# Involution block on one core: the convolution in eight parts of two channel groups by four images, in place of four parts of one group by eight images

## The chip, the cores and the metric

The kernel runs on one core of a Trainium2 chip. The metric is device time in microseconds (us). Engines in the text: PE (matmuls), PEld (its weight loads), DVE (vector), ACT (scalar), POOL (GpSimd), SP (here it only issues DMAs). A core has 16 DMA engines that move what all queues ask for.

## The reference

The input x has 16 images of 64 channels, 56 x 56 pixels. The block adds an involution (a 7 x 7 convolution whose weights are made per pixel from the normalised input) and then a mixture of experts, two of eight per token.

```
r   = relu(batchnorm(conv1x1(ln_c(x), w1) + b1))          # 16 channels
ker = conv1x1(r, w2) + b2                                 # 16 groups x 49 taps per pixel
for i in range(7):
    for j in range(7):                                    # 4 channels of a group share a tap
        out += shifted(ln_c(x), i, j) * ker[:, :, i*7 + j]
x = x + out
t = tokens(x)                                             # 50176 tokens of 64
top_w, top_i = top_k(ln_t(t) @ Wg + bg, 2)                # 8 experts
t = t + sum over the two of w * (gelu(ln_t(t) @ W1[e] + b1[e]) @ W2[e] + b2[e])
```

All arithmetic is float32.

## The kernel before

Four stages follow one another: normalisation (it writes the normalised maps to a DRAM tensor `xs`, the reduced channels to `rs`, and the tap weights to `vf`), the convolution with the gate, the experts, and a merge. The change is in the first two.

**Convolution.** `STEPS` = 64 steps, t = 0 to 63. A step takes one of the four quarters (`QUARTERS`: upper or lower half of the rows, even or odd images; 16 steps each) and one channel group g = t % 16 (4 channels) of the quarter's 8 images. SP loads per step one `band` tile (`load_band`, L846: 119 partitions of 238 floats, the group's taps from `vf`; the source is written as 17 rows by 7 columns of 952 bytes) and three strips of the maps (`load_maps`, L856: 112 partitions of 8192 bytes each at L867, and a seventeenth row of 7 partitions at L870 for the first strip). There are 3 band buffers (`BR`) and 8 strip buffers (`XR`); a load waits until PE has read the buffer's last content. Strips and band of the first kind are split into two float32r parts: the high parts on ACT (L965 band, L972 maps), the low parts on DVE (L1144, L1147, in `low_parts` after the fourth unit of the step before). PE's `filters` then makes 8 units of matmuls (L1069 to L1075), DVE's `weigh` multiplies each unit with `r_all` (L1158), PE's `sums` adds them up (L1088), ACT evacuates (`evacuate`, L984) and stores to `co` (L990, one DMA of 128 partitions).

**Gate.** `CHUNKS` = 56 chunks of 896 tokens, 14 per quarter. `step_of(n)` puts chunk n at step 16 * (n // 14 + 1) + 2 + n % 14: a quarter's chunks are gated while the next quarter is convolved, and those of the last quarter in steps 66 to 79, after the convolution. A chunk is loaded by SP (`load_chunk`, from x and `co`; the first of a quarter waits until all stores of that quarter have landed), multiplied on PE (`unit`, L1103, in the step after the second unit, so PE waits there for the load), read out by ACT and ranked on DVE. Two chunks make a batch (28 in all), ranked one step after its second chunk and placed another step later; then POOL writes the batch's rows to `token_rows` with 14 indirect DMAs (L951). POOL does nothing else there, but for 28 earlier DMAs that fill `packs`.

Every queue works in order of the program: what stands behind a waiting instruction waits too. SP's order per step t is band and strips of step t + 1, then the chunk of step t.

The first stage stores the normalised maps with `xs_map` (L265, L316) inside a hardware loop (`rounds`, L320) on SP.

Of the kernel before, what the change touches and what calls it, by code (L numbers as in the profile page):

```python
# [79 lines left out]
QUARTERS = ((0, 0), (0, 1), (1, 0), (1, 1))  # L80
HALF = HALF_ROWS * W
QUARTER_CHUNKS = CHUNKS // len(QUARTERS)
BAND_LEAST = [min(IN0[r] - MROWS * m for r in strips for m in STRIP_BLOCKS[r]) for strips in STRIP_SETS]
BN = MF + MROWS * F

# [95 lines left out]
def norm_stage(nc, x, conv_w1, conv_b1, gamma, beta, conv_w2, conv_b2, xs, rs, ones_rows, vf,  # L181
# [11 lines left out]
    with ExitStack() as ctx:  # L193
# [68 lines left out]
        counted = sem("counted")  # L262
        packed = sem("packed")

        xs_map = xs[0:XS_SIZE].rearrange("(i h c x) -> i c h x", i=PARITY, h=H, c=C)  # L265
        vf_map = vf[:].rearrange("(g j t f) -> g j t f", g=G, j=K, t=TL)
        w2_map = conv_w2.rearrange("(i j g) c -> i g j c", i=K, j=K)
        b2_map = conv_b2.rearrange("(i j g u) -> i g j u", i=K, j=K, u=1)
# [7 lines left out]
        @block.sync  # L276
        def _(sp):
            x_pairs = x.rearrange("(p i) c h w -> p (i c) (h w)", i=PARITY)
            def load(pair):

                if pair >= 2:
                    sp.wait_ge(x_in[pair % 2], pair // 2 * 16)
                sp.dma_start(xin[:, pair, :], x_pairs[pair]).then_inc(x_in[pair % 2], 16)

            load(0)
            load(1)


            sp.wait_ge(cleared, 3)
            sp.dma_start(vf[:].rearrange("(p x) -> p x", p=P), zeros[:, :]).then_inc(blanks_done, 16)  # L290
            sp.dma_start(xs[XS_SIZE:XS_SIZE + WP].rearrange("(a x) -> a x", a=1),
                         zeros[0:1, 0:WP]).then_inc(blanks_done, 16)
            sp.dma_start(ones_rows.rearrange("j (x w) -> (j x) w", w=P8 * W),
                         ones[:, :]).then_inc(blanks_done, 16)
            load(2)
            load(3)

            def step(it, k):
                if isinstance(it, int) and it == 0 and k % 2 == 0:
# [14 lines left out]

                for i in range(PARITY):
                    sp.dma_start(xs_map[i][:, PAIR_ROWS * u:PAIR_ROWS * (u + 1), bass.ds(j * 2 * WP, 2 * WP)],  # L316
                                 xpad[u][C * i:C * (i + 1), :, :, :].rearrange("c h p w -> c h (p w)")
                                 ).then_inc(xs_out[u], 16)

            rounds(sp, STEPS, PER, 3, step)  # L320

            sp.wait_ge(blanks_done, 3 * 16)
            sp.wait_ge(filters_out, 2 * K * 16)
            for i in range(2):
                sp.wait_ge(rs_out[i], STEPS // 4 * 4 * 16)
            for u in range(UNITS):
                sp.wait_ge(xs_out[u], P8 // 2 * PARITY * 16)
# [366 lines left out]
def conv_gate_stage(nc, x, xs, rs, ones_rows, vf, co, affine, pick, tables, token_rows, tile_table,  # L694
# [8 lines left out]
    with ExitStack() as ctx:  # L703
# [7 lines left out]
        xq = [sb(f"xq{i}", [KP, XN]) for i in range(XR)]  # L711
        xq_hi = [sb(f"xq_hi{i}", [KP, XN], F32R) for i in range(2)]
        xq_lo = [sb(f"xq_lo{i}", [KP, XN], F32R) for i in range(2)]
        band = [sb(f"band{i}", [KP, BN]) for i in range(BR)]
        band_hi = [sb(f"band_hi{i}", [KP, BN], F32R) for i in range(2)]
        band_lo = [sb(f"band_lo{i}", [KP, BN], F32R) for i in range(2)]
# [99 lines left out]
        def quarter_of(t):  # L816
            return QUARTERS[t // G]

        def strip_of(t, i):
            return STRIP_SETS[quarter_of(t)[0]][i]  # L820

# [8 lines left out]
        R_STEPS = (0, 0, 4, 9, 25)  # L830
        R_NEED = (0, 0, G, 2 * G, 3 * G)
        def step_of(n):
            return G * (n // QUARTER_CHUNKS + 1) + 2 + n % QUARTER_CHUNKS

        def placing_step(b):
            return step_of(BATCH * b + BATCH - 1) + 2
# [8 lines left out]
        @block.sync  # L845
        def _(sp):  # L846
            def load_band(t):
                s, g = quarter_of(t)[0], t % G
                if t >= BR:
                    sp.wait_ge(b_lo, t - BR + 1)  # L850
                    sp.wait_ge(z_done, NU * (t - BR) + NU)
                src = bass.AP(vf, g * V_G + (TAP0 + PAD - (MROWS - 1) + BAND_LEAST[s]) * F,
                              [[F, max(KR)], [V_J, K], [1, BN]])
                sp.dma_start(band[t % BR][:, :], src).then_inc(band_in[t % BR], 16)

            def load_maps(t, i):  # L856
                n = GS * t + i
                slot, r = n % XR, strip_of(t, i)
                if n >= XR:
# [5 lines left out]
                par, g, top = quarter_of(t)[1], t % G, IN0[r]  # L865
                base = (par * H + top) * XS_H + g * XN
                sp.dma_start(xq[slot][0:16 * K, :],  # L867
                             bass.AP(xs, base, [[XS_H, 16], [1, K], [1, XN]])).then_inc(x_in[slot], 16)
                if i == 0:
# [12 lines left out]
                             ).then_inc(r_in[part], 16)  # L882

            def load_chunk(n):
                if n % QUARTER_CHUNKS == 0:
                    for i in range(2):
                        sp.wait_ge(ob_out[i], (n // QUARTER_CHUNKS + 1) * G // 2 * 16)
                if n >= XC:
                    sp.wait_ge(unit_done, n - XC + 1)
                for img, at, to, size in pieces(n):  # L890
                    sp.dma_start(xc[n % XC][0:C, to:to + size],
                                 x[img].rearrange("c h w -> c (h w)")[:, at:at + size]).then_inc(xc_in[n % XC], 16)
                    sp.dma_start(xc[n % XC][C:2 * C, to:to + size],
                                 conv_run(co, img, at, size)).then_inc(xc_in[n % XC], 16)
# [64 lines left out]
        @block.scalar  # L959
        def _(act):  # L960
            def split_band(t):
                act.wait_ge(band_in[t % BR], (t // BR + 1) * 16)
                if t >= 2:
                    act.wait_ge(z_done, NU * (t - 2) + LAST_UNIT[0] + 1)
                nc.scalar.activation(band_hi[t % 2][:, :], band[t % BR][:, :], ACT.Copy).then_inc(b_hi, 1)  # L965

            def split_maps(t):
                slot = GS * t % XR
# [11 lines left out]

            def evacuate(t):
                act.wait_ge(summed, t + 1)
                act.wait_ge(ob_out[t % 2], t // 2 * 16)
# [4 lines left out]
                dst = co[s, par, t % G].rearrange("i d q (h w) -> (q h) (i d) w", w=W)  # L988
                act.wait_ge(ob_done, t + 1)
                act.dma_start(dst, ob[t % 2][:, :].rearrange("p (e w) -> p e w", w=W)).then_inc(ob_out[t % 2], 16)  # L990

            def take_unit(n):
                b, k = divmod(n, BATCH)
# [56 lines left out]
        def _(pe):  # L1050
            def filters(t, u):
# [10 lines left out]
                for lot, (m, q) in enumerate(parts):  # L1062
                    zt = z_ps[(NU * t + u) % 3][0:MF, lot, 0:CN]
                    at = window(t, m, r)
                    if i == 0:
                        maps = [part[t % 2][rows_in, :].rearrange("p (d i w) -> p d i w", d=D, i=P8)[
                            :, :, 2 * q:2 * q + 2, 0:W] for part in (xq_hi, xq_lo)]
                        hi, lo = (part[t % 2][rows_in, at:at + MF] for part in (band_hi, band_lo))
# [69 lines left out]
        def _(dve):  # L1138
            def low_parts(t):
                slot = GS * t % XR  # L1140
                dve.wait_ge(b_hi, t + 1)
                if t >= 2:
                    dve.wait_ge(z_done, NU * (t - 2) + LAST_UNIT[0] + 1)
                nc.vector.tensor_tensor(band_lo[t % 2][:, :], band[t % BR][:, :],  # L1144
                                        band_hi[t % 2][:, :].bitcast(F32), ALU.subtract).then_inc(b_lo, 1)
                dve.wait_ge(x_hi, t + 1)
                nc.vector.tensor_tensor(xq_lo[t % 2][:, :], xq[slot][:, :],  # L1147
                                        xq_hi[t % 2][:, :].bitcast(F32), ALU.subtract).then_inc(x_lo, 1)
# [1 line left out]
            def weigh(t, u):  # L1150
                i, ((m, q), (m1, _)) = UNITS_OF[quarter_of(t)[0]][u]
                par = quarter_of(t)[1]
                dve.wait_ge(z_done, NU * t + u + 1)
                if m1 != m:
                    by = r_all[:, m:m + 2, par, 2 * q * W:2 * (q + 1) * W]
                else:
                    by = r_all[:, m, par, 2 * q * W:2 * (q + 2) * W].rearrange("p (m x) -> p m x", m=2)
# [554 lines left out]
```

## Time and profile before

| | us |
|---|---|
| median of 3 runs | 2265.68 |
| lowest and highest | 2265.55, 2266.97 |
| profiled execution | 2268.61 |
| its span, first to last instruction | 2266.7 |
| busy PE, DVE, ACT, POOL in the span | 1932.9, 1516.8, 785.9, 970.3 |
| mean granted clock of PE | 0.914 |

The profiled execution is 2.9 us above the median; 1.9 us of it lie outside its span. In a row of the profile an engine's idle time before an instruction stands in brackets with the instruction or DMA that ended it. SP rows are DMA issues: their duration is the time that the issue itself took on the queue. DMA share is the mean busy share of the 16 DMA engines, so a single busy engine shows as 0.06. Granted clock 1.00 is 2.4 GHz, 0.50 is 1.2 GHz.

### The profile page before, as it was taken

Reading aid. Unit: us, or ns where it says so; the run is one execution under the profiler, and the core shown is the slowest. Engines: PE = TensorE matmul, PEld = TensorE weight load, DVE = VectorE, ACT = ScalarE, POOL = GpSimd, SP = SyncE. Lnnn points to the kernel's source line nnn. Section 1 sums busy time; section 2 is a strip of 40 time slices with the busy share of each in tenths; the row PEclk is TensorE's granted clock in tenths of the full one; section 3 lists DMA queues with packets and bytes.
Section 4 is the critical chain, followed back from the end, with each engine's and each line's share of the span. In section 5 each row is a group of like instructions: output and inputs, shape, how many; then the busy total and the mean of one; then the engine's idle time right before and its main releaser. Section 6 shows DMA issues by size and latency. Waiting matters only on the chain. (4 is left out here: it accounts for less than half of the span.)

```text
span 2266.7 us, 32062 instructions
## 1 busy us (share of the span) xinstructions
PE 1932.9 (85%) x10208; PEld 1045.7 (46%) x10208; DVE 1516.8 (67%) x2682; ACT 785.9 (35%) x1382; POOL 970.3 (43%) x1038
## 2 busy tenths in 40 slices
PE   8975898887999999999999995307999999999945
PEld 5753444344555545555555554303444444444424
DVE  4444566565888877989878897634666666666634
ACT  4431111111223222232223323214666666666620
POOL 8001000100225350443505346773777777777740
PEclk9987999898999999999999995557999999999977
DMA  9767888887888777888778853234666566666439
GB/s 301 163 131 191 201 203 205 205 200 196 211 214 212 208 204 207 226 222 211 203 195 230 215 134 105 72 93 124 176 168 169 166 167 170 166 166 174 117 120 349
DMA packets 265820, 418.92 MB, mean 185 GB/s; under 512 B 116224, under 2 KB 188452, under 8 KB 242685
## 3 DMA queue, kind: packets, MB, share of 16 engines
q1 hardware_dynamic: 160701, 348.14, 57.8%
q0 software_dynamic: 32352, 39.58, 6.5%
q10 hardware_dynamic: 72608, 29.25, 5.5%
q8 instruction: 79, 1.29, 0.2%
q14 instruction: 80, 0.66, 0.1%
HBM read 337.34 MB, written 89.60 MB: 188 GB/s over the span
## 5 line engine op out<-in xcount | busy, mean ns | idle before, releaser
L951 POOL DMA_INDIRECT token_rows<-gate_rows,gate_index x392 | 414.9, 1059 | 663.4 <-DVE gate_index L1280 549.7
L1158 DVE TENSOR_TENSOR prod<-z_ps,r_all 119x896 f32<-119x896 f32 x512 | 543.5, 1083 | 130.8 <-PE z_ps L1071 100.8
L1474 POOL DMA_INDIRECT mixed<-exp_mix,exp_xt x474 | 478.0, 1008 | 175.3 <-issue 132.1
L1075 PE MATMUL z_ps<-xq,band 112*119 112x448 f32 x1024 | 442.4, 568 | 68.8 <-DVE prod L1158 68.7
L1492 ACT ACTIVATE exp_hid<-exp_h_ps,exp_pack 128x384 f32<-128x384 f32 x632 | 329.6, 574 | 242.2 <-PE exp_h_ps L1528 242.2
L1075 PEld LDWEIGHTS z_ps<-xq,band 112*119 112x119 f32 x1024 | 183.7, 189 | 277.3 <-issue 178.6
L1528 PE MATMUL exp_h_ps<-exp_tok,exp_pack 64*128 64x384 f32 x1264 | 248.9, 512 | 10.7 <-issue 10.4
L984 ACT ACTIVATE ob<-o_ps 128x448 f32<-128x448 f32 x64 | 34.8, 544 | 609.6 <-PE o_ps L1088 609.6
L1088 PE MATMUL o_ps<-prod,pick 119*32 119x448 f32 x2048 | 240.1, 562 | 1.2 <-DVE prod L1158 0.3
L1536 PE MATMUL exp_y_ps<-exp_hid,exp_pack 128*64 128x384 f32 x1264 | 238.8, 499 | 0.0
L1069 PE MATMUL z_ps<-xq_hi,band_hi 119*119 119x448 f32 x512 | 207.5, 405 | 23.7 <-DVE xq_lo L1147 20.7
L1570 DVE COPY exp_tok<-exp_x_ps 64x384 f32<-64x384 f32 x158 | 86.8, 550 | 166.8 <-PE exp_x_ps L1516 164.1
L1070 PE MATMUL z_ps<-xq_lo,band_hi 119*119 119x448 f32 x512 | 190.1, 371 | 0.0
L1071 PE MATMUL z_ps<-xq_hi,band_lo 119*119 119x448 f32 x512 | 189.2, 370 | 0.0
L1147 DVE TENSOR_TENSOR xq_lo<-xq,xq_hi 119x2048 fp32r<-119x2048 f32 x64 | 146.3, 2285 | 56.6 <-ACT xq_hi L972 56.6
L1103 PE MATMUL u_ps<-moe_gate_rhs,gate_xc 128*128 128x72 f32 x784 | 120.3, 317 | 74.0 <-issue 46.1
L1069 PEld LDWEIGHTS z_ps<-xq_hi,band_hi 119*119 119x119 f32 x512 | 94.4, 184 | 133.4 <-issue 115.9
L1103 PEld LDWEIGHTS u_ps<-moe_gate_rhs,gate_xc 128*128 128x128 f32 x784 | 116.7, 231 | 82.2 <-issue 52.0
L1528 PEld LDWEIGHTS exp_h_ps<-exp_tok,exp_pack 64*128 64x128 f32 x1264 | 111.2, 187 | 79.1 <-issue 39.3
L1576 DVE TENSOR_SCALAR exp_ysb<-exp_y_ps,exp_pack 64x384 f32<-64x384 f32 x158 | 98.6, 624 | 69.0 <-PE exp_y_ps L1536 68.1
L972 ACT ACTIVATE xq_hi<-xq 119x2048 fp32r<-119x2048 f32 x64 | 121.6, 1900 | 54.5 <-DMA xq<-xs 54.4
L1516 PE MATMUL exp_x_ps<-ident,exp_xt 128*64 128x128 f32 x474 | 82.8, 284 | 51.6 <-DMA exp_xt<-token_rows 51.6
(196 smaller groups left out, 2019.1 us busy)
## 6 DMA issues: line engine op xcount, KB each, us to landing
xq<-xs SPq DMA_DIRECT2D x192, 896.0 KB
exp_pack<-packs SPq DMA_DIRECT2D x158, 258.5 KB
exp_xt<-token_rows SPq DMA_DIRECT2D x158, 120.0 KB
xs<-xpad SPq DMA_DIRECT2D x32, 448.0 KB, 5.9
co<-ob ACTq DMA_DIRECT2D x64, 224.0 KB, 16.7
xin<-in_x_dram SPq DMA_DIRECT2D x8, 1568.0 KB, 11.2
merge_yt<-mixed ACTq DMA_DIRECT2D x28, 448.0 KB, 6.0
mixed<-exp_mix,exp_xt POOLq DMA_INDIRECT x474
```

The costliest lines, as they stand in the source:

```text
L951: pool.indirect_dma_start(out=token_rows[:, :], out_offset=bass.IndirectOffsetOnAxis(ap=index[b % RR][:, j:j + 1], axis=0), in_=rows[b % R ...
L1069: nc.tensor.matmul(zt, hi, maps[0], start=True, stop=False)
L1070: nc.tensor.matmul(zt, hi, maps[1], start=False, stop=False)
L1071: mm = nc.tensor.matmul(zt, lo, maps[0], start=False, stop=True)
L1075: mm = nc.tensor.matmul(zt, band[t % BR][rows_in, at:at + MF], maps, start=True, stop=True)
L1088: mm = nc.tensor.matmul(o_ps[32 * q:32 * (q + 1), 0:CN], pick[:, cols], prod[(NU * t + u) % PR][:, lot, :], start=i == 0 and lot == 0, sto ...
L1103: mm = nc.tensor.matmul(u_ps[:, GATE_COLS * j:GATE_COLS * (j + 1)], xc[n % XC][:, P * j:P * (j + 1)], tab.gate_rhs[:, :], start=True, stop ...
L1158: nc.vector.tensor_tensor(prod[(NU * t + u) % PR][:, :, :].rearrange("p m (d x) -> p m d x", d=D), z_ps[(NU * t + u) % 3][0:MF, :, 0:CN].r ...
L1474: pool.indirect_dma_start(out=mixed[:, :], out_offset=bass.IndirectOffsetOnAxis(ap=xt[t % XT][:, j, ROW_ID:ROW_ID + 1].bitcast(U32), axis= ...
L1492: nc.scalar.activation(hid[n % 8][:, :], h_ps[n % HT][:, 0:N], ACT.Gelu, bias=pack[t % WT][:, at:at + 1]).then_inc(gelu_done, 1)
L1528: nc.tensor.matmul(h_ps[n % HT][:, 0:N], pack[t % WT][half, P * blk:P * (blk + 1)], tok[t % 3][half, :], start=True, stop=True).then_inc(h ...
L1536: mm = nc.tensor.matmul(y_ps[t % 2][C * e:C * (e + 1), 0:N], pack[t % WT][:, at:at + C], hid[(t * 4 + 2 * blk + e) % 8][:, :], start=blk = ...
```

## The change

A quarter is halved into two sides of four images, so there are eight parts of 8 steps and 7 chunks each. A step takes two channel groups (twins) of four images; it has as many output values as before. `xs` is laid out so that a strip's 8192 bytes hold 8 channels of 4 images. A step now needs the bands of two groups: two band DMAs of the old size into a tile twice as wide, and the high and low split of 476 columns in place of 238. Chunk n is gated at step 8 * (n // 7 + 1) + 2 + n % 7: the first chunk moves from step 18 to step 10, the last from step 79 to step 72. The store to `co` becomes two DMAs of 64 partitions. Waits on all stores of a part come eight times in place of four. The loop of SP in the first stage is written out.

```diff
+SIDES = 2
+SIDE_CHUNKS = QUARTER_CHUNKS // SIDES
+TWINS = G // 2
+SIDE_X = P8 // SIDES * WP
...
-        xs_map = xs[0:XS_SIZE].rearrange("(i h c x) -> i c h x", i=PARITY, h=H, c=C)
+        xs_map = xs[0:XS_SIZE].rearrange("(i h a c x) -> i a c h x", i=PARITY, h=H, a=SIDES, c=C)
...
-                    sp.dma_start(xs_map[i][:, PAIR_ROWS * u:PAIR_ROWS * (u + 1), bass.ds(j * 2 * WP, 2 * WP)],
+                    at = j % (P8 // SIDES // 2) * 2 * WP
+                    sp.dma_start(xs_map[i, j // (P8 // SIDES // 2)][:, PAIR_ROWS * u:PAIR_ROWS * (u + 1), at:at + 2 * WP],
...
-            rounds(sp, STEPS, PER, 3, step)
+            for n in range(STEPS + 3):
+                step(*divmod(n, PER))
...
-        band = [sb(f"band{i}", [KP, BN]) for i in range(BR)]
+        band = [sb(f"band{i}", [KP, 2, BN]) for i in range(BR)]
...
+        def side_of(t):
+            return t // TWINS % SIDES
...
-            return G * (n // QUARTER_CHUNKS + 1) + 2 + n % QUARTER_CHUNKS
+            return TWINS * (n // SIDE_CHUNKS + 1) + 2 + n % SIDE_CHUNKS
...
-                src = bass.AP(vf, g * V_G + (TAP0 + PAD - (MROWS - 1) + BAND_LEAST[s]) * F,
-                              [[F, max(KR)], [V_J, K], [1, BN]])
-                sp.dma_start(band[t % BR][:, :], src).then_inc(band_in[t % BR], 16)
+                for twin in range(2):
+                    g = t % TWINS * 2 + twin
+                    src = bass.AP(vf, g * V_G + (TAP0 + PAD - (MROWS - 1) + BAND_LEAST[s]) * F,
+                                  [[F, max(KR)], [V_J, K], [1, BN]])
+                    sp.dma_start(band[t % BR][:, twin, :], src).then_inc(band_in[t % BR], 16)
...
-                base = (par * H + top) * XS_H + g * XN
+                base = (par * H + top) * XS_H + side_of(t) * C * SIDE_X + t % TWINS * XN
...
-                if n % QUARTER_CHUNKS == 0:
+                if n % SIDE_CHUNKS == 0:
                     for i in range(2):
-                        sp.wait_ge(ob_out[i], (n // QUARTER_CHUNKS + 1) * G // 2 * 16)
+                        sp.wait_ge(ob_out[i], (n // SIDE_CHUNKS + 1) * TWINS // 2 * 2 * 16)
...
-                nc.scalar.activation(band_hi[t % 2][:, :], band[t % BR][:, :], ACT.Copy).then_inc(b_hi, 1)
+                nc.scalar.activation(band_hi[t % 2][:, :, :], band[t % BR][:, :, :], ACT.Copy).then_inc(b_hi, 1)
...
+                lots = slice(CH // SIDES * side_of(t), CH // SIDES * (side_of(t) + 1))
+                for twin in range(2):
+                    dst = co[s, par, t % TWINS * 2 + twin][:, :, lots].rearrange("i d q (h w) -> (q h) (i d) w", w=W)
+                    act.dma_start(dst, ob[t % 2][P // 2 * twin:P // 2 * (twin + 1), :]
+                                  .rearrange("p (e w) -> p e w", w=W)).then_inc(ob_out[t % 2], 16)
...
-                        maps = xq[n % XR][rows_in, :].rearrange("p (d i w) -> p d i w", d=D, i=P8)[
-                            :, :, 2 * q:2 * q + 2, 0:W]
-                        mm = nc.tensor.matmul(zt, band[t % BR][rows_in, at:at + MF], maps, start=True, stop=True)
+                        maps = xq[n % XR][rows_in, :].rearrange("p (e d i w) -> p e d i w", e=2, d=D, w=WP)[
+                            :, twin, :, images, 0:W]
+                        mm = nc.tensor.matmul(zt, band[t % BR][rows_in, twin, at:at + MF], maps, start=True, stop=True)
...
-                nc.vector.tensor_tensor(band_lo[t % 2][:, :], band[t % BR][:, :],
-                                        band_hi[t % 2][:, :].bitcast(F32), ALU.subtract).then_inc(b_lo, 1)
+                nc.vector.tensor_tensor(band_lo[t % 2][:, :, :], band[t % BR][:, :, :],
+                                        band_hi[t % 2][:, :, :].bitcast(F32), ALU.subtract).then_inc(b_lo, 1)
```

## Rows read from the trace of the kernel before

**Rows 1.** Windows: start:end us, length, busy per engine (count), granted clock, DMA share, GB/s.

```profile
230.00:490.00 260.00, 221.98 (x997) 110.44 (x989) 153.71 (x139) 43.53 (x44) 17.22 (x24) 0.91 0.83 202
900.00:1079.00 179.00, 170.45 (x884) 95.26 (x882) 158.55 (x287) 52.60 (x80) 76.14 (x70) 1.00 0.82 216
...
1365.00:1531.40 166.40, 53.72 (x232) 50.27 (x228) 93.03 (x325) 40.49 (x75) 126.17 (x126) 0.51 0.32 92
1531.40:2266.70 735.30, 652.44 (x3672) 308.50 (x3672) 449.06 (x846) 386.97 (x791) 478.00 (x474) 0.94 0.61 172
```

**Rows 2.** One line's instructions: L984's evacuations, one per step, then L990's landing times.

```profile
L984 ACT ACTIVATE ob<-o_ps x64: 543/544/547, 215.8 to 1365.3; 128x448 f32<-128x448 f32 x64
...
DMA to landing us min/median/max: 2.6/16.7/19.3
```

**Rows 3.** Lines of DVE, 900 to 1079 us: count, busy us, mean ns, idle before.

```profile
L1158 DVE TENSOR_TENSOR prod<-z_ps,r_all 119x896 f32<-119x896 f32 x80 | 84.3, 1080 | 0.0
L1147 DVE TENSOR_TENSOR xq_lo<-xq,xq_hi 119x2048 fp32r<-119x2048 f32 x10 | 22.8, 2282 | 0.0
...
L1144 DVE TENSOR_TENSOR band_lo<-band,band_hi 119x238 fp32r<-119x238 f32 x10 | 4.0, 396 | 0.0
```

**Rows 4.** Waits of ACT, 230 to 490 us: total us, times, longest.

```profile
ACT xq_hi L972 <- DMA xq<-xs: 35.2, 13, 4.3
ACT band_hi L965 <- DMA band<-vf: 30.2, 6, 6.9
```

**Rows 5.** Waits of SP's queue, 900 to 1079 us, same columns.

```profile
SPq L851 <- PE z_ps L1075: 98.0, 10, 11.5
```

**Rows 6.** Timeline of SP from the convolution's first load: start us, duration us, what.

```profile
167.63 0.74 SPq L854 DMA_DIRECT2D band<-vf  x1
168.42 1.00 SPq L867 DMA_DIRECT2D xq<-xs  x1
169.47 0.54 SPq L870 DMA_DIRECT2D xq<-xs  x1
170.05 1.35 SPq L867 DMA_DIRECT2D xq<-xs  x2
171.44 0.65 SPq L854 DMA_DIRECT2D band<-vf  x1
172.13 17.20 SPq L867 DMA_DIRECT2D xq<-xs  x1
```

**Rows 7.** Timeline of ACT over the same first loads, idle before in brackets.

```profile
178.85 0.40 ACT L965 ACTIVATE band_hi<-band 119x238 fp32r<-119x238 f32 x1 [17.46 <-DMA band<-vf]
184.41 1.91 ACT L972 ACTIVATE xq_hi<-xq 119x2048 fp32r<-119x2048 f32 x1 [5.16 <-DMA xq<-xs]
...
197.10 0.40 ACT L965 ACTIVATE band_hi<-band 119x238 fp32r<-119x238 f32 x1 [8.23 <-DMA band<-vf]
201.48 1.91 ACT L972 ACTIVATE xq_hi<-xq 119x2048 fp32r<-119x2048 f32 x1 [3.98 <-DMA xq<-xs]
```

**Rows 8.** Windows with one DMA engine at work, columns as in rows 1.

```profile
186.80:190.00 3.20, 1.21 (x3) 1.11 (x4) 1.85 (x1) 1.68 (x2) 0.00 (x0) 0.50 0.06 25
1007.50:1008.50 1.00, 1.00 (x10) 0.16 (x8) 0.97 (x3) 0.00 (x0) 0.00 (x0) 1.00 0.06 22
1008.50:1009.50 1.00, 1.00 (x8) 0.74 (x5) 1.00 (x2) 0.55 (x1) 0.91 (x1) 1.00 0.07 24
```

**Rows 9.** DMA packets between 555.77 and 556.73 us.

```profile
DMA packets 25, 0.03 MB, mean 32 GB/s; under 512 B 0, under 2 KB 24, under 8 KB 24
```

**Rows 10.** Timeline of SP in a gated step.

```profile
1004.46 0.66 SPq L854 DMA_DIRECT2D band<-vf  x1
1005.16 3.68 SPq L867 DMA_DIRECT2D xq<-xs  x1
```

**Rows 11.** POOL's lines after the convolution, 1365 to 1532 us.

```profile
L951 POOL DMA_INDIRECT token_rows<-gate_rows,gate_index x126 | 126.2, 1001 | 54.5 <-issue 38.1 <-DVE gate_index L1280 16.3
```

**Rows 12.** Timeline of PE at the first gated chunk.

```profile
537.66 3.26 PE L1103 MATMUL u_ps<-moe_gate_rhs,gate_xc 128*128 128x72 f32 x14 [11.07 <-DMA gate_xc<-co]
```

More of the change, by code:

```diff
@@ L298, in step @@
             def step(it, k):
-                if isinstance(it, int) and it == 0 and k % 2 == 0:
+                if it == 0 and k % 2 == 0:
                     load(4 + k // 2)
@@ L713, in conv_gate_stage @@
         xq_lo = [sb(f"xq_lo{i}", [KP, XN], F32R) for i in range(2)]
-        band = [sb(f"band{i}", [KP, BN]) for i in range(BR)]
-        band_hi = [sb(f"band_hi{i}", [KP, BN], F32R) for i in range(2)]
-        band_lo = [sb(f"band_lo{i}", [KP, BN], F32R) for i in range(2)]
+        band = [sb(f"band{i}", [KP, 2, BN]) for i in range(BR)]
+        band_hi = [sb(f"band_hi{i}", [KP, 2, BN], F32R) for i in range(2)]
+        band_lo = [sb(f"band_lo{i}", [KP, 2, BN], F32R) for i in range(2)]
         prod = [sb(f"prod{i}", [MF, 2, CN]) for i in range(PR)]
@@ L847, in load_band @@
             def load_band(t):
-                s, g = quarter_of(t)[0], t % G
+                s = quarter_of(t)[0]
                 if t >= BR:
@@ L864, in load_maps @@
                         sp.wait_ge(z_done, NU * was + LAST_UNIT[kind] + 1)
-                par, g, top = quarter_of(t)[1], t % G, IN0[r]
-                base = (par * H + top) * XS_H + g * XN
+                par, top = quarter_of(t)[1], IN0[r]
+                base = (par * H + top) * XS_H + side_of(t) * C * SIDE_X + t % TWINS * XN
                 sp.dma_start(xq[slot][0:16 * K, :],
@@ L961, in split_band @@
             def split_band(t):
-                act.wait_ge(band_in[t % BR], (t // BR + 1) * 16)
+                act.wait_ge(band_in[t % BR], (t // BR + 1) * 2 * 16)
                 if t >= 2:
                     act.wait_ge(z_done, NU * (t - 2) + LAST_UNIT[0] + 1)
-                nc.scalar.activation(band_hi[t % 2][:, :], band[t % BR][:, :], ACT.Copy).then_inc(b_hi, 1)
+                nc.scalar.activation(band_hi[t % 2][:, :, :], band[t % BR][:, :, :], ACT.Copy).then_inc(b_hi, 1)
             def split_maps(t):
@@ L982, in evacuate @@
                 act.wait_ge(summed, t + 1)
-                act.wait_ge(ob_out[t % 2], t // 2 * 16)
+                act.wait_ge(ob_out[t % 2], t // 2 * 2 * 16)
                 nc.scalar.activation(ob[t % 2][:, :].rearrange("p (i d w) -> p d i w", i=2, d=D),
@@ L987, in evacuate @@
                 s, par = quarter_of(t)
-                dst = co[s, par, t % G].rearrange("i d q (h w) -> (q h) (i d) w", w=W)
                 act.wait_ge(ob_done, t + 1)
-                act.dma_start(dst, ob[t % 2][:, :].rearrange("p (e w) -> p e w", w=W)).then_inc(ob_out[t % 2], 16)
+                lots = slice(CH // SIDES * side_of(t), CH // SIDES * (side_of(t) + 1))
[3 more added lines that the diff above has]
+                                  .rearrange("p (e w) -> p e w", w=W)).then_inc(ob_out[t % 2], 16)
             def take_unit(n):
@@ L1064, in filters @@
                     at = window(t, m, r)
+                    twin, side_lot = divmod(q, CH // SIDES)
+                    images = slice(2 * side_lot, 2 * side_lot + 2)
                     if i == 0:
-                        maps = [part[t % 2][rows_in, :].rearrange("p (d i w) -> p d i w", d=D, i=P8)[
-                            :, :, 2 * q:2 * q + 2, 0:W] for part in (xq_hi, xq_lo)]
-                        hi, lo = (part[t % 2][rows_in, at:at + MF] for part in (band_hi, band_lo))
+                        maps = [part[t % 2][rows_in, :].rearrange("p (e d i w) -> p e d i w", e=2, d=D, w=WP)[
+                            :, twin, :, images, 0:W] for part in (xq_hi, xq_lo)]
+                        hi, lo = (part[t % 2][rows_in, twin, at:at + MF] for part in (band_hi, band_lo))
                         nc.tensor.matmul(zt, hi, maps[0], start=True, stop=False)
@@ L1152, in weigh @@
                 par = quarter_of(t)[1]
+                first_image = P8 // SIDES * side_of(t) + 2 * (q % (CH // SIDES))
                 dve.wait_ge(z_done, NU * t + u + 1)
                 if m1 != m:
-                    by = r_all[:, m:m + 2, par, 2 * q * W:2 * (q + 1) * W]
+                    by = r_all[:, m:m + 2, par, first_image * W:(first_image + 2) * W]
                 else:
-                    by = r_all[:, m, par, 2 * q * W:2 * (q + 2) * W].rearrange("p (m x) -> p m x", m=2)
+                    by = r_all[:, m, par, first_image * W:(first_image + 4) * W].rearrange("p (m x) -> p m x", m=2)
                 nc.vector.tensor_tensor(prod[(NU * t + u) % PR][:, :, :].rearrange("p m (d x) -> p m d x", d=D),
```

## The prediction

> **What bounds the kernel now.** I read the windows by stage first. The span has four parts: normalisation up to the first band load at 167.63 us [rows 6], 64 convolution steps whose evacuations run from 215.8 to 1365.3 us, so (1365.3 - 215.8) / 63 = 18.25 us per step [rows 2], a stretch of 166.4 us in which the gate finishes alone and PE is busy for 53.72 us [rows 1], and experts with merge, 735.30 us, which the change does not touch [rows 1].
>
> The stretch after the convolution is POOL's. Its 126 indirect DMAs take 126.2 us and the idle time before them is 54.5 us, of which 38.1 is its own issue and only the first 16.3 (mostly before the stretch) a wait for DVE [rows 11]. So one DMA costs (126.2 + 38.1) / 126 = 1.30 us, a batch of 14 costs 18.3 us, and nine batches stand there one behind another.
>
> In the gated steps, 900 to 1079 us, DVE looks like the bound: its big multiplications, 80 of them, start without idle time, and so do both low splits [rows 3]. SP waits there for free buffers, 98.0 us in ten steps [rows 5], so loads are ahead of the work. In the steps before the gate starts it is the other way: ACT waits for strips 35.2 us and for bands 30.2 us [rows 4].
>
> The third thing to see is the one that decides: **how a band travels.** It is 119 packets of 952 bytes where a strip is 112 of 8192, an eighth of the bytes, yet it is the slow one. At the start nothing else of the convolution is in flight. SP issues band 0, the four DMAs of step 0's strips, band 1, and then step 1's first strip, whose issue alone takes 17.20 us [rows 6]. ACT gets band 0 at 178.85, strip 0 at 184.41, band 1 only at 197.10, strip 1 at 201.48 [rows 7]: 25.7 us for a band that was issued 3.8 us behind its forerunner. That is a single file: band, strips, band, strips. At 186.80 to 190.00, inside this wait, the DMA share is 0.06, one engine of 16, while the others stand still; the same share shows in the gated steps, at 1007.5 to 1009.5, just when the issue of a strip is held on SP for 3.68 us [rows 8, 10]. And 24 packets of a band, with nothing else moving, take 0.96 us, 40 ns each, in a row [rows 9]. So I read: all 119 packets of every band go through one DMA engine, always the same one, and that engine also carries its sixteenth of every strip, chunk and store. Call it the lane. The lane is full in both kinds of steps: where the gate runs it still works alone when the next loads are issued.
>
> The Trainium skill states a rule for this (DMA: Bandwidth & Descriptors, section "Why a DMA increments its semaphore by 16 and not by 1"): a DMA of SP runs on the largest number of engines up to 16 that divides the slowest dimension on both sides, the lowest-numbered ones. 17 rows and 119 partitions have no common divisor of that size but 1, so by it both twin bands go to the same engine; by the opposite reading, 119 packets spread over 16 engines, a second band would cost 8 x 40 ns = 0.3 us. The share of 0.06 agrees with the rule.
>
> **The change part by part.**
>
> *Second band DMA per step.* 119 more packets of 952 bytes on the lane, 64 times. Lower bound: 119 x 40 ns = 4.8 us, the lane alone [rows 9]. Upper bound from the start: between band 0 and band 1 the lane carries 22 strip pieces and a band in 197.10 - 178.85 = 18.25 us; the eight pieces of strip 1 take 201.48 - 197.10 = 4.38, so 0.55 each, 22 of them 12.1, and the band 6.2 [rows 7]. I take 5.2, near the lower bound, because the other 15 engines have finished their share when the added packets run. Since the lane has no room, this is step time: 64 x 5.2 = +333 us (307 to 397). A step would then last some 23 us.
>
> *Loads are no longer ahead.* Now the last strips wait in SBUF for their turn; then the convolution ends sooner after its last load. Taking the 9.8 us that SP waits for buffers per gated step as the lead [rows 5], -8 us.
>
> *Splits of 476 columns.* DVE: from 396 ns at 238 to 2282 ns at 2048 columns is 1.04 ns per column [rows 3], +0.25 us per step; ACT: (1.91 - 0.40) / 1810 us, +0.2 us [rows 7]. Priced at 0: in a step of 23 us DVE with its 158.55 us in ten steps has 7 us spare [rows 1]. Without that cover it is 64 x 0.25 = 16 us.
>
> *Chunks gated earlier.* At the end of the convolution, before: the last placed batch is that of chunks 38 and 39 (step 61, ranked 62, placed 63), batch 19, so POOL has batches 19 to 27 to write, nine. After: chunks 44 and 45 sit in step 61, batch 22, and six are left. The first of them need nothing new, and the chunk that must wait for the last stores (chunk 49, in batch 24) is wanted 2 x 18.3 us later. -3 x 18.3 = -55 us. The seven chunks go into steps 10 to 16 where DVE and PE have the spare time of a 23 us step; their pieces on the lane, eight per chunk, are in the 18.25 us average that the sum starts from, at the same rate.
>
> *More waits for a part's stores.* SP waits eight times in place of four, with the next step's loads queued behind it. The store awaited is three steps old and lands within 19.3 us at most [rows 2], less than one new step: 0. The first chunk of all once made PE wait 11.07 us [rows 12]; such a wait at each part's start is inside a lane-bound step, where PE has some 5 us spare: 0 to 6 x 6 = 36 us, taken as 0.
>
> *Stores as two DMAs of 64 partitions:* the same pieces, one more issue on ACT's queue, which is busy 52.60 of 179 us [rows 1]: 0. *Layout of `xs`, weights, SP's loop written out:* the same packets and instructions, 0, give or take 2 us. POOL's `packs` DMAs stand at the steps where they were.
>
> Sum against the profiled execution: 2268.6 + 333 - 8 - 55 = 2539. The median lies 2.9 us under it: **2535 us**, some 12% slower.
>
> **The rivals.**
>
> *A. The lane has room or the second band takes another one.* For it: in gated steps DVE never waits for a load [rows 3] and SP waits for buffers [rows 5]. Against it: the held issue and the share of 0.06 [rows 8, 10]. Then the tail's 55 us remain, less 0.25 us x 54 gated or nearly DVE-bound steps = 14 and four more first-chunk waits of about 3 us (rows 12 shows the worst): 2268.6 - 55 + 14 + 12 - 3 = 2237. This is the one on the other side; it decides if a band costs the lane under 55 / 64 = 0.9 us.
>
> *B. Part of the cost hides.* If the lane's 17.9 us in gated steps are partly drawn out by DVE's pace, with a real need of 15 to 16 us, a step becomes 20.5 to 21 us: about 64 x 2.8 = 179 in place of 333, 2380.
>
> *C. The lane's delay spreads.* A chunk's load stands on the lane behind the next step's two bands, and PE waits for it in the middle of a step; PE's clock was at 0.51 in the stretch where it mostly waited [rows 1], and a step with waits of several us may run in part at 1.2 GHz. If PE's chain, not the lane, then sets the step, at 26 us: + 64 x 2.5 = 160, about 2690.
>
> *D. The tail does not shrink* because the chunks, not POOL, set it: 2590, within the main forecast's range.
>
> **How the numbers follow.** Main forecast with D 0.74; A 0.09; B 0.10; C 0.06; no change 0.01 (the gain of the tail just eaten). The main case runs from 2268.6 + 307 - 66 = 2510 to 2268.6 + 397 - 0 = 2665. Giving B part of its weight, the range is 2420 to 2665. Faster by over 0.2% (what a measurement of this kernel can tell from none) 0.09, within 0.2% 0.01, slower 0.90.
>
> **What would show it.** Right: steps of 22 to 25 us; ACT waiting for band or strips in nearly every step, DVE's multiplications with idle time in all of them; windows of 5 us per step with a DMA share of 0.06; mean share in the convolution falling from 0.82 to about 0.65; issues of strips held 5 us or more; POOL's stretch after the convolution about 112 us. Wrong: DVE still without idle time in the gated steps, steps of 18 us, bands landing 6 us after issue.

## The result, and the profile after

The changed kernel takes 2610.53 us (median of four, 2606.44 to 2621.30), against 2266.32 (2265.55 to 2268.44) for the kernel before: a ratio of 1.1524, 95% interval 1.1493 to 1.1556. The forecast was 2535, in a range of 2420 to 2665. The profiled execution of after took 2621.3 us, span 2619.5; before's span was 2266.7.

The path of the time, from the evacuation line of each kernel, the first band load and the end of POOL's last indirect DMA of rows in each trace (us):

| point | before | after | stretch up to it longer by |
|---|---|---|---|
| first band load issued | 167.6 | 174.2 | 6.6 |
| first evacuation | 215.8 | 230.9 | 8.5 |
| last evacuation | 1365.3 | 1772.7 | 392.3 |
| end of POOL's last row DMA | 1531.4 | 1883.9 | -54.9 |
| end of the span | 2266.7 | 2619.5 | 0.3 |

The 63 steps between the evacuations last (1772.7 - 230.9) / 63 = 24.47 us each where they lasted 18.25 [rows 2]. First the same views as in [rows 1, 2, 11]: the evacuation line (ns of one, then first and last start), the windows by stage (busy time and count per engine, granted clock, DMA share, GB/s), and POOL after the convolution.

```profile
L995 ACT ACTIVATE ob<-o_ps x64: 544/546/550, 230.9 to 1772.7; 128x448 f32<-128x448 f32 x64
...
230.00:490.00 260.00, 185.58 (x772) 93.92 (x766) 118.23 (x106) 39.20 (x41) 13.06 (x20) 0.83 0.63 162
900.00:1200.00 300.00, 238.55 (x1072) 139.87 (x1072) 194.35 (x334) 68.79 (x96) 72.87 (x70) 0.85 0.65 164
...
1774.50:1883.90 109.40, 27.82 (x118) 26.06 (x118) 58.08 (x210) 24.03 (x44) 83.86 (x84) 0.51 0.33 95
1883.90:2619.50 735.60, 656.54 (x3672) 311.57 (x3672) 449.20 (x846) 387.55 (x791) 479.86 (x475) 0.93 0.62 172
...
L962 POOL DMA_INDIRECT token_rows<-gate_rows,gate_index x84 | 83.9, 999 | 51.8 <-DVE gate_index L1297 26.3 <-issue 25.5
```

No compute engine became the bound: in the gated stretch PE, DVE and ACT are all less busy than before [rows 1], and the mean DMA share went down, from 0.82 to 0.65. POOL has 84 indirect DMAs to issue after the convolution where it had 126 [rows 11].

What holds the steps is seen where nothing else runs, at the start. SP's timeline of after (start, duration of the issue), then two windows, then ACT's timeline:

```profile
174.22 1.81 SPq L865 DMA_DIRECT2D band<-vf  x2
176.07 7.27 SPq L878 DMA_DIRECT2D xq<-xs  x1
...
185.17 14.30 SPq L865 DMA_DIRECT2D band<-vf  x2
199.52 5.47 SPq L878 DMA_DIRECT2D xq<-xs  x1
...
196.50:199.50 3.00, 0.00 (x0) 0.00 (x0) 1.58 (x1) 3.00 (x3) 0.00 (x0) 0.50 0.06 25
199.50:205.00 5.50, 4.64 (x13) 4.03 (x14) 1.80 (x2) 0.44 (x1) 0.00 (x0) 0.50 0.07 23
...
213.15 0.60 ACT L976 ACTIVATE band_hi<-band 119x476 fp32r<-119x476 f32 x1 [13.21 <-DMA band<-vf]
217.54 1.91 ACT L983 ACTIVATE xq_hi<-xq 119x2048 fp32r<-119x2048 f32 x1 [3.79 <-DMA xq<-xs]
```

For 8.5 us one DMA engine of 16 works (0.06 to 0.07) at 23 to 25 GB/s, which is 952 bytes in some 40 ns, while the issue of the next pair of bands is held 14.30 us on SP and ACT waits 13.21 us for a band. The window of this kind in before was 3.2 us long [rows 8]. In a gated step of after one engine works alone for 6 us:

```profile
1030.00:1036.00 6.00, 6.00 (x31) 2.62 (x31) 6.00 (x10) 1.03 (x1) 0.00 (x0) 1.00 0.07 22
```

In the gated steps the wait stands elsewhere than before. Waits of 900 to 1200 us (total us, times, longest), then DVE's and PE's lines from the page of after:

```profile
DVE prod L1175 <- PE z_ps L1087: 65.5, 11, 16.9
PE u_ps L1119 <- DMA gate_xc<-co: 57.3, 11, 12.6
ACT xq_hi L983 <- DMA xq<-xs: 4.0, 1, 4.0
ACT band_hi L976 <- DMA band<-vf: 1.6, 1, 1.6
...
L1175 DVE TENSOR_TENSOR prod<-z_ps,r_all 119x896 f32<-119x896 f32 x512 | 547.1, 1085 | 422.6 <-PE z_ps L1087 390.1
L1119 PE MATMUL u_ps<-moe_gate_rhs,gate_xc 128*128 128x72 f32 x784 | 169.7, 403 | 298.3 <-DMA gate_xc<-co 275.0
```

DVE's multiplications, which started without idle time before [rows 3], now wait for PE, and PE waits for the gate's chunk, which SP issues behind the bands.

### The profile page after: what moved, and what is told of

Its sections match the earlier page's. It is cut to its first block and busy times, and to the rows that moved or that the text cites. A ratio compares the mean times of both kernels' runs of the same rounds, so it can differ in the third digit from the quotient of the medians.

```text
span 2619.5 us, 32031 instructions
## 1 busy us (share of the span) xinstructions
PE 2061.1 (79%) x10208; PEld 1146.2 (44%) x10208; DVE 1531.2 (58%) x2682; ACT 802.6 (31%) x1382; POOL 961.3 (37%) x1038
## 5 line engine op out<-in xcount | busy, mean ns | idle before, releaser
L962 POOL DMA_INDIRECT token_rows<-gate_rows,gate_index x392 | 404.4, 1032 | 924.8 <-DVE gate_index L1297 811.8
L1091 PE MATMUL z_ps<-xq,band 112*119 112x448 f32 x1024 | 469.6, 600 | 75.8 <-DVE prod L1175 75.8
L1119 PE MATMUL u_ps<-moe_gate_rhs,gate_xc 128*128 128x72 f32 x784 | 169.7, 403 | 298.3 <-DMA gate_xc<-co 275.0
L1091 PEld LDWEIGHTS z_ps<-xq,band 112*119 112x119 f32 x1024 | 203.1, 207 | 295.4 <-issue 200.7
L1119 PEld LDWEIGHTS u_ps<-moe_gate_rhs,gate_xc 128*128 128x128 f32 x784 | 159.0, 308 | 317.9 <-DMA gate_xc<-co 292.9
L1085 PE MATMUL z_ps<-xq_hi,band_hi 119*119 119x448 f32 x512 | 227.6, 445 | 25.7 <-DVE xq_lo L1163 25.7
L1086 PE MATMUL z_ps<-xq_lo,band_hi 119*119 119x448 f32 x512 | 207.9, 406 | 0.0
L1087 PE MATMUL z_ps<-xq_hi,band_lo 119*119 119x448 f32 x512 | 206.8, 404 | 0.0
L1587 DVE COPY exp_tok<-exp_x_ps 64x384 f32<-64x384 f32 x158 | 86.8, 549 | 167.0 <-PE exp_x_ps L1533 165.2
L1085 PEld LDWEIGHTS z_ps<-xq_hi,band_hi 119*119 119x119 f32 x512 | 106.2, 207 | 132.3 <-issue 115.7
L953 POOL DMA_DIRECT2D packs<-firsts x14 | 8.9, 637 | 349.5 <-PE z_ps L1091 349.5
```

The lines of the kernel that those rows point to most:

```text
L962: pool.indirect_dma_start(out=token_rows[:, :], out_offset=bass.IndirectOffsetOnAxis(ap=index[b % RR][:, j:j + 1], axis=0), in_=rows[b % R ...
L1091: mm = nc.tensor.matmul(zt, band[t % BR][rows_in, twin, at:at + MF], maps, start=True, stop=True)
L1119: mm = nc.tensor.matmul(u_ps[:, GATE_COLS * j:GATE_COLS * (j + 1)], xc[n % XC][:, P * j:P * (j + 1)], tab.gate_rhs[:, :], start=True, stop ...
```

## The experiments

The prediction's theory is called *the lane*: all 119 packets of a band go through one DMA engine, that engine is full, and so every added packet is step time. Its rivals: the engine has room (A), a part of the cost hides (B), the loss comes by way of PE's wait for chunks (C).

### Spread the band over the engines

In before and in after, each band is loaded in two pieces, sixteen rows of seven partitions and the seventeenth row; the same bytes land in the same places.

```diff
-                sp.dma_start(band[t % BR][:, :], src).then_inc(band_in[t % BR], 16)
+                sp.dma_start(band[t % BR][0:16 * K, :],
+                             bass.AP(vf, at, [[F, 16], [V_J, K], [1, BN]])).then_inc(band_in[t % BR], 16)
+                sp.dma_start(band[t % BR][16 * K:17 * K, :],
+                             bass.AP(vf, at + 16 * F, [[V_J, K], [1, BN]])).then_inc(band_in[t % BR], 16)
```

Of the kernel before:

> The kernel before, with its one band per step loaded in two pieces, 16 rows of 7 (112 partitions) and the seventeenth row (7 partitions), in place of 17 rows of 7 at once; the same bytes. Theory (every packet of a band goes through one DMA engine, and that engine is full): issues of strips are no longer held for 11 to 18 us in the steps before the gate, ACT no longer waits for bands there, those steps fall from 18.4 to about 15.5 us and the first steps start some 15 us earlier; gated steps stay at 17.9 us, where DVE has no idle time. Together 2200 to 2235 us. Rival (the DMA engines as a whole, or the bytes, are the limit): 2266 us, no change.

Of the kernel after, both twins:

> The changed kernel, with each of the two bands of a step loaded in the same two pieces (16 rows of 7, and one row of 7). Theory (the 344 us come from the second band on the one engine): the steps fall from 24 to 18 us or less, DVE is without idle time again, POOL's stretch after the convolution stays at 112 us; 2160 to 2240 us, faster than the kernel before. Rival (the order in eight parts itself, with chunk loads that PE waits for in every step and a lower granted clock, makes it slow; or the added bytes do): above 2450 us.

Before spread: 2183.61 us, ratio 0.9639 (0.9612 to 0.9665). After spread: 2219.18, ratio 0.9793 (0.9776 to 0.9811), which is 391 us under after. The evacuation line of each, with before spread's first loads on SP and its windows:

```profile
L986 ACT ACTIVATE ob<-o_ps x64: 544/545/547, 210.6 to 1284.1; 128x448 f32<-128x448 f32 x64
...
177.52 0.56 SPq L869 DMA_DIRECT2D xq<-xs  x1
...
230.00:490.00 260.00, 253.68 (x1223) 131.70 (x1222) 185.49 (x168) 48.85 (x54) 17.23 (x24) 0.99 0.98 244
850.00:1060.00 210.00, 199.88 (x1026) 110.76 (x1025) 182.65 (x316) 58.15 (x86) 91.17 (x84) 0.99 0.83 217
```

```profile
L997 ACT ACTIVATE ob<-o_ps x64: 544/546/550, 204.7 to 1373.9; 128x448 f32<-128x448 f32 x64
```

Step 1's first strip, whose issue took 17.20 us before [rows 6], is issued in 0.56. In the steps without gate the mean DMA share rises from 0.83 [rows 1] to 0.98: now all engines work together. So the lane held the kernel before, too, and rival A falls. Before spread is faster than the 2200 to 2235 us that were expected: the gated steps were to stay as they were, but from evacuation 17 to the last they shortened as well, from 840.0 us to 810.9. After spread is inside its range, and 36 us slower than before spread; that is followed up below.

The Trainium skill (DMA: Bandwidth & Descriptors, section "Why a DMA increments its semaphore by 16 and not by 1") has a DMA of SP run on the largest number of engines up to 16 that divides the slowest dimension on both sides; by it 17 rows into 119 partitions go to one engine and 16 rows into 112 partitions to 16. The DMA share of 0.06 and the 80 us of the spread load agree.

### A second band without the eight parts

Before, with the same band loaded a second time into a spare tile that nobody reads: once in the old form, once spread, once only 51 of its packets (17 rows by 3).

```diff
                 sp.dma_start(band[t % BR][:, :], src).then_inc(band_in[t % BR], 16)
+                sp.dma_start(spare[t % BR][:, :], src).then_inc(band_in[t % BR], 16)
...
-                act.wait_ge(band_in[t % BR], (t // BR + 1) * 16)
+                act.wait_ge(band_in[t % BR], (t // BR + 1) * 2 * 16)
```

> The kernel before, with each band loaded a second time in the same form into a spare tile that nobody reads; order, parts, chunks and splits are those of before. Theory: 119 more packets on the one engine cost 5.2 to 6.3 us in every step, so 2590 to 2670 us. Rival (the order in eight parts makes the change slow): within 1% of 2266 us.

> The kernel before, with each band loaded a second time into a spare tile, this time in pieces of 16 rows by 7 and one row by 7. The first load of the band keeps its form. Theory: the added 119 packets are 8 per engine, 0.3 to 0.6 us per step on each: 2266 to 2310 us. Rival (the added bytes or the added DMA, not the one engine, cost the time): 2590 us or more, as with the load in the old form.

> As e3_before_second_band, with 51 packets in the second load (17 rows of 3) in place of 119. Theory (the one engine pays per packet): 51/119 of the 341 us of e3_before_second_band, 2390 to 2440 us. Rival (an added DMA on the queue costs a fixed time, or only the order on the queue matters): within 2% of e3_before_second_band, 2555 to 2660 us, or of no second load, 2250 to 2300 us.

Each ran once: 2607.30 us in the old form (before on that chip 2263.53, +344), 2275.62 spread (+12), and 2408.91 with 51 packets (before there 2263.02, +146). The same bytes cost 344 us through one engine and 12 us through all. Per packet that is 344 / 64 / 119 = 45 ns and 146 / 64 / 51 = 45 ns. The queue lines of the page, before with the second band and then after (packets, MB, share of 16 engines), and the former's evacuations and waits from 900 to 1200 us:

```profile
q1 hardware_dynamic: 168381, 355.39, 51.7%
...
L986 ACT ACTIVATE ob<-o_ps x64: 543/544/547, 226.6 to 1697.8; 128x448 f32<-128x448 f32 x64
...
DVE prod L1160 <- PE z_ps L1073: 80.9, 14, 16.7
PE u_ps L1105 <- DMA gate_xc<-co: 50.3, 11, 12.2
```

```profile
q1 hardware_dynamic: 168381, 355.39, 52.5%
```

SP's queue moves as many packets in both kernels, and the second band alone brings a loss of the same size and the same pair of waits. That both kernels lose 344 us is chance: after also loses and saves by its eight parts, as shown below.

### The eight parts without the second band

After, with the load of twin 1's band left out: its half of the tile is zeroed once by DVE, so half of the channel groups get no taps; every other instruction is there.

```diff
-                for twin in range(2):
+                for twin in range(1):
...
-                act.wait_ge(band_in[t % BR], (t // BR + 1) * 2 * 16)
+                act.wait_ge(band_in[t % BR], (t // BR + 1) * 16)
```

> The changed kernel with the band of the second twin left out (its half of the tile is set to zero once, so half of the groups have no taps); everything else is as changed: eight parts, chunk steps, splits of 476 columns, two stores. Theory (the second band on the one DMA engine is what the change lost): steps fall from 24 to about 18.5 us, 2220 to 2290 us. Rival (the order in eight parts, its chunk loads and its clock): above 2450 us.

2256.79 us in a single run, beside 2260.02 for before. So without the second band's packets the change is worth nothing or 3 us. Its evacuations:

```profile
L998 ACT ACTIVATE ob<-o_ps x64: 544/546/550, 214.0 to 1405.7; 128x448 f32<-128x448 f32 x64
```

Their stretch is 1191.7 us where before's is 1149.5: the eight parts themselves cost some 42 us in the convolution, which eats most of what they save behind it.

### The chunk ahead of the bands

After, with SP's two loads of a step exchanged, for rival C.

```diff
-                if t + 1 < STEPS:
-                    load_step(t + 1)
                 if t in chunk_at:
                     load_chunk(chunk_at[t])
+                if t + 1 < STEPS:
+                    load_step(t + 1)
```

> The changed kernel with SP issuing the chunk of step t ahead of the band and strips of step t + 1, not behind them. Bytes and packets are the same. Theory (the one DMA engine alone sets the step, and PE's waits for chunks only show it): PE's waits for chunks shrink, waits for bands and strips take their place, 2590 to 2630 us. Rival (PE's wait in the middle of a step, with the clock falling, adds the 1.1 us per step by which the step came out longer than forecast): 2530 to 2560 us.

2607.89 us in a single run: no change. Waits from 900 to 1200 us:

```profile
ACT band_hi L976 <- DMA band<-vf: 44.5, 7, 6.9
ACT xq_hi L983 <- DMA xq<-xs: 40.3, 13, 4.4
PE z_ps L1091 <- DVE prod L1175: 76.7, 7, 12.2
```

PE's waits for chunks are gone, and ACT's waits for bands and strips stand in their place. PE still waits in the middle of steps, now for DVE (76.7 us, longest 12.2). Whoever is last in the lane waits; who that is does not set the step. Rival C falls as far as it rests on the wait for chunks; what PE's lower clock in these steps (0.85, against 1.00 before [rows 1]) adds was not measured apart.

### What the eight parts lose with the lane free

After spread is 36 us slower than before spread. Its traces show a chain across two engines: DVE's `gate_rstd` waits for ACT's `gate_std` 23.5 us from 850 to 1060 us (longest 6.0), in before spread 17.1 (longest 3.4). That step of ACT (`deviation`) stands behind the evacuation, the store's two issues and both splits. Two edits of after spread: the store issued behind the deviation, and the deviation put first in ACT's step.

```diff
+            def store(t):
                 s, par = quarter_of(t)
                 act.wait_ge(ob_done, t + 1)
...
                 if t in rank_at:
                     deviation(rank_at[t])
+                if 1 <= t <= STEPS:
+                    store(t - 1)
```

```diff
             for t in range(LAST):
+                if t in rank_at:
+                    deviation(rank_at[t])
                 if 1 <= t <= STEPS:
                     evacuate(t - 1)
...
-                if t in rank_at:
-                    deviation(rank_at[t])
                 if t in chunk_at:
                     take_unit(chunk_at[t])
```

> As e2_after_spread, with ACT issuing the two stores of a step behind the splits and the deviation, not ahead of them. Theory (with the loads out of the way DVE waits for ACT's deviation, 23.5 us in five batches against 17.1 in e1_before_spread, and the second store's issue stands ahead of it): some 1.5 us per batch in 25 batches come back, 2170 to 2200 us. Rival (the wider splits, or the operands' strides, are what e2_after_spread loses against e1_before_spread): 2219 us, no change.

> As e2_after_spread, with ACT computing the deviation of a batch at the start of the step, ahead of evacuation, stores and splits. Theory: DVE's wait for it (4.4 to 6 us per batch) goes, up to 25 times, until PE is the bound at 33 to 34 us per two steps: 2120 to 2175 us, faster than e1_before_spread too. Rival (PE is the bound already): 2190 us or more.

Store late: 2176.73 us, ratio 0.9615 (0.9574 to 0.9656), 42 us under after spread (39 when each is taken against before on its own chip). Deviation first: 2123.52, ratio 0.9380 (0.9340 to 0.9421), another 53 us less and far under both kernels. In it DVE's waits from 900 to 1100 us are these three, and none is for ACT:

```profile
DVE prod L1177 <- PE z_ps L1089: 7.1, 7, 1.7
DVE prod L1177 <- issue: 2.4, 2, 1.2
DVE prod L1177 <- PE z_ps L1093: 1.0, 2, 0.5
```

Its partner is before spread with the same edit of ACT's order, four parts against eight with nothing else between them:

> As e1_before_spread (the kernel before in four parts, with the band in two pieces), with ACT computing a batch's deviation at the start of the step. It is the partner of e8_after_spread_deviation_first: the two differ by the eight parts alone. Theory (with the one engine free, the eight parts are worth the three batches of POOL that leave the end, 55 us): 2165 to 2190 us. Rival (the gain of e8_after_spread_deviation_first is that of the deviation alone, and the eight parts give nothing): 2110 to 2140 us.

2129.05 us, ratio 0.9385 (0.9350 to 0.9421). The expectation of 2165 to 2190 was wrong and its rival came true: the two cannot be told apart, so with the lane free no gain of the eight parts can be seen. Their profiles show why, eight parts first: the evacuations, those around steps 9 to 17, PE's wait for chunks from 360 to 500 us (in the four-part kernel two of ACT's waits there), and the window from the last evacuation to the end of POOL's last row DMA.

```profile
L997 ACT ACTIVATE ob<-o_ps x64: 544/546/551, 210.1 to 1277.0; 128x448 f32<-128x448 f32 x64
L997 ACT ACTIVATE ob<-o_ps x9: 544/545/551, 352.6 to 516.4; 128x448 f32<-128x448 f32 x9
PE u_ps L1121 <- DMA gate_xc<-co: 23.9, 3, 12.4
1277.00:1388.10 111.10, 29.44 (x132) 27.54 (x132) 59.73 (x213) 23.09 (x43) 83.83 (x84) 0.52 0.34 93
```

```profile
L986 ACT ACTIVATE ob<-o_ps x64: 543/544/547, 208.0 to 1239.5; 128x448 f32<-128x448 f32 x64
L986 ACT ACTIVATE ob<-o_ps x9: 543/544/544, 346.1 to 482.7; 128x448 f32<-128x448 f32 x9
411.28 0.54 ACT L986 ACTIVATE ob<-o_ps 128x448 f32<-128x448 f32 x1 [17.25 <-DMA co<-ob]
440.00 0.54 ACT L986 ACTIVATE ob<-o_ps 128x448 f32<-128x448 f32 x1 [25.48 <-DMA co<-ob]
1239.50:1406.50 167.00, 53.55 (x228) 50.29 (x228) 92.63 (x324) 38.90 (x73) 126.99 (x126) 0.51 0.32 92
```

The eight parts save 167.0 - 111.1 = 55.9 us behind the convolution and lose 1066.9 - 1031.5 = 35.4 between the evacuations, 27.2 of it in steps 9 to 17 (163.8 against 136.6), where the first part's chunks now stand and PE waits 23.9 us for them. The loss is larger than that. In steps 9 to 17 the four-part kernel has no gate yet and runs the same code as before spread, which took 119.1 us for them; the other 17.5 most likely belong to this execution, the longest of the four (2120.93 to 2142.43), in which ACT sat idle 17.25 and 25.48 us until a store had landed. Without them the parts lose 44.7 us there and 53 in all, against the 55.9 saved, and the 16.9 us between the two profiles are gone. The medians differ by 5.5; how much of that is real stays open.

## Why the prediction was right, point by point

**The mechanism** was right: the second band is paid in full, on one DMA engine. Rival A (2237) fell with the spread load and the second band, B (2380) with the second band's full price, C, as far as it rests on the wait for chunks, with the exchange of chunk and bands.

**Second band, +333.** The clean measure is before with the second band, whose first load was issued at 172.3 us: from there to the last evacuation 1525.5 us, before 1365.3 - 167.6 = 1197.7. That is 327.8 / 64 = 5.12 us a load, against the 5.2 taken between 4.8 and 6.2. The reason given for lying near the lower bound, that the other engines have finished, is what the window of 0.06 at 23 to 25 GB/s shows.

**Loads no longer ahead, -8.** No row shows such a gain; it is not seen apart from the terms around it.

**The eight parts in the convolution, priced at 0: the term that was mis-sized.** Take after against before with the second band. From first load to last evacuation it is 1772.7 - 174.2 = 1598.5 against 1525.5, so +73, twice the upper end given (36 us of first-chunk waits). The evacuations of the two kernels split it: 9.4 up to step 9, 210.0 - 187.9 = 22.1 in steps 9 to 17, and 41.5 in the rest. Evacuations around steps 9 to 17 and what the DMA engines moved between them, with PE's waits there, in after; the same without waits in before with the second band; and the evacuations of after with the chunk ahead of the bands:

```profile
L995 ACT ACTIVATE ob<-o_ps x9: 544/545/546, 442.3 to 652.3; 128x448 f32<-128x448 f32 x9
DMA packets 17503, 36.17 MB, mean 172 GB/s; under 512 B 9871, under 2 KB 12327, under 8 KB 14619
PE u_ps L1119 <- DMA gate_xc<-co: 54.5, 7, 16.1
```

```profile
L986 ACT ACTIVATE ob<-o_ps x9: 544/544/546, 431.0 to 618.9; 128x448 f32<-128x448 f32 x9
DMA packets 14722, 30.95 MB, mean 165 GB/s; under 512 B 8966, under 2 KB 10901, under 8 KB 11905
```

```profile
L995 ACT ACTIVATE ob<-o_ps x9: 544/544/546, 436.8 to 648.3; 128x448 f32<-128x448 f32 x9
```

The step that failed is "the seven chunks go into steps 10 to 16 where DVE and PE have the spare time", with the chunks' pieces on the lane taken as being in the 18.25 us average. PE had the time, and waited in all seven steps for a chunk, up to 16.1 us. But the wait only shows the loss: with the chunk ahead of the bands PE waits for no chunk there, and these steps still last 648.3 - 436.8 = 211.5 us. The average does not cover them either. It holds 42 chunks in 64 steps, and after has 48; and where before with the second band moves 3.9 MB a step both here (30.95 / 8) and in the gated steps behind, after moves 36.17 / 8 = 4.5 here, since the gate's transfers come on top of what these steps carried already. An estimate: a sixteenth of the 5.22 MB more is 0.33 MB, and at the 0.55 us that the prediction read for a strip piece of 8192 bytes the lane needs 22 us for it, which is the 22.1 measured. That is worked out, not tried: no run took the chunks or POOL's `packs` transfers out of these steps.

With the lane free the same steps lose more, 162.9 us in after spread (first line below) against 119.1 in before spread. There the DMA engines together are full before anything is added (a share of 1.02 in the window of before spread), and the 5.5 MB that after spread moves on top (35.87 against 30.38) would take some 21 us at the 255 GB/s of that window; the rest is open.

```profile
L997 ACT ACTIVATE ob<-o_ps x9: 544/544/546, 355.2 to 518.1; 128x448 f32<-128x448 f32 x9
```

```profile
L986 ACT ACTIVATE ob<-o_ps x9: 545/546/547, 354.2 to 473.2; 128x448 f32<-128x448 f32 x9
354.20:473.20 119.00, 119.00 (x577) 62.25 (x577) 88.46 (x81) 23.77 (x25) 6.26 (x8) 1.00 1.02 255
```

The 41.5 us of steps 17 to 63, 0.9 a step, were not isolated. A loss of this size does not need a full lane: with the lane free after spread loses 855.8 - 810.9 = 44.9 us there against before spread, and only with the deviation first does that shrink to 760.6 - 756.8 = 3.8. DVE's waits for `gate_std` are longer in after, too, 100.6 us from there on against 72.7 in before with the second band. So ACT's order may be the cause under the full lane as well; no run changed it there.

**Two stores, one more issue on ACT: 0.** Not tried under the full lane. With the lane free, moving them behind the deviation gained some 40 us, so the price of 0 does not hold there. Here the prediction asked how busy ACT's queue is and should have asked who waits for what stands behind the issue.

**Three POOL batches leave the end, -55.** Measured -54.9, in a stretch of 111.2 us (forecast 112). The same came out with the lane free (-55.9). Rival D fell.

**The start.** The first load came 6.6 us later; the last section has the reason. Together: 327.8 + 73.0 - 54.9 + 6.6 + 0.3 = 352.8 us, the difference of the spans. The forecast missed the median by 75 us and the profiled execution, from which these terms are read, by 83 (2621.3 - 2538.6): 73 for the parts, 8 for the gain that did not show, 7 for the start, less 5 for the second band. The range held because it was wide enough for a term that it did not contain.

**The signs.** Steps of 22 to 25 us, a share of 0.65, issues held over 5 us and POOL's stretch came as said; the windows with a single engine at work lasted 8.5 us at the start and 6 in the gated step shown. ACT's wait for bands and strips showed up before the gate (47.1 and 40.4 us from 230 to 490), but in gated steps it was 5.6 us in 300: there PE's chunk, issued last, took the wait. The exchanged loads brought it back to ACT. A sign should have named the lane's last passenger, not one engine.

## What to carry to other kernels

A DMA share of 0.06 together with an issue that is held for microseconds was here the sign that one engine carries a whole transfer. Its packets of 952 bytes cost 40 to 45 ns each as long as that engine was full, and splitting the odd dimension (17 rows into 16 and 1) alone took 80 us off the kernel before; so look for that before anything else is weighed. When work is moved from a tail into a loop, price the transfers that it brings into the loop's steps, and not only its busy time; and before a wait is called the cause, move it, as the exchange of chunk and bands did. An issue on a queue that is hardly busy can still cost, so ask of each issue who waits behind it.

## What was not expected of the hardware

The time of the first band load varied with no edit near it, from 166.5 to 172.5 us in the six kernels with four parts and from 165.7 (after spread) to 174.2 (after) in the six with eight. From 16 to 35 us, in the normalisation, PE is busy throughout in a late one (after, first row) and in an early one (after spread, second row), but with 77 and 141 matmuls; the third row is the kernel with the chunk ahead of the bands (first load at 171.0 us):

```profile
16.00:35.00 19.00, 19.00 (x77) 14.14 (x78) 4.60 (x8) 6.83 (x10) 17.13 (x37) 1.00 0.95 307
```

```profile
16.00:35.00 19.00, 18.54 (x141) 13.52 (x141) 8.03 (x14) 10.75 (x17) 17.13 (x37) 1.00 1.02 310
```

```profile
16.00:35.00 19.00, 19.00 (x79) 13.78 (x79) 4.62 (x8) 6.16 (x9) 17.25 (x36) 0.52 1.00 301
```

That is 247 ns each against 131. The column of the granted clock says 1.00 for the first two, but in after the records of the clock begin, at 1.00, only at about 35.5 us, and in after spread at 16.0. In the third they begin earlier, and there the granted clock is 0.52 with as few matmuls as in after. So PE most likely ran at 1.2 GHz in after up to there and at 2.4 GHz from there on, and the 6.6 us at the start belong to the execution and not to the change.

The order of ACT's queue was worth more than the eight parts: putting one activation of 0.31 us per two chunks (`deviation`, with a table load of 1.28 us) first in ACT's step took 2183.61 to 2129.05 us with four parts and 2219.18 to 2123.52 with eight.
